# Sorting stage of a graph network kernel: one-hot compares in 16 bit, rows laid by value and then tile

## The reference

```python
edge_index = jnp.stack([src, dst])
x = x + _L0_gnn_ref(_layernorm(x, axis=-1), edge_index, ...)
...
x = x + _L1_gnn_ref(_layernorm(x, axis=-1), edge_index, edge_attr_256, ...)   # sums by dst
...
x = x + _L2_gnn_ref(_layernorm(x, axis=-1), edge_attr_20, ..., edge_index)    # sums by src
...
x = x + _L3_gnn_ref(_layernorm(x, axis=-1), edge_index, ...)                  # softmax and sums by dst
```

## Time and profile before

| | us |
|---|---|
| timed runs | 4594.09, 4598.11, 4608.26 (median 4598.11) |
| span of the profiled execution, first to last instruction | 4590.3 |
| median above that span | 7.8 |
| sorting stage, from the start to the next stage's first loads | 0 to 487.7 |
| first stretch, counting list 0 | 20.8 to 101 |
| second stretch, ranking list 0 and counting list 1 | 113 to 318 |
| third stretch, ranking list 1 | 322 to 460 |
| POOL's scatters in this stage | 118.9 to 483.0 |

### The profile page before, as it was taken

One profiled execution on the slowest core, in us unless ns is written; L12 is line 12 of the kernel. 1 busy time (PEld: TensorE's weight loads), 2 busy tenths in 40 slices (PEclk: granted clock), 3 DMA queues, 4 the chain that ended last, 5 costly groups with the idle time before them and its releaser, 6 DMA issues. The chain is left out here.

```text
span 4590.3 us, 75478 instructions
## 1 busy us (share of the span) xinstructions
PE 3650.0 (80%) x20805; PEld 2939.0 (64%) x20890; DVE 2883.1 (63%) x6152; ACT 1718.4 (37%) x3863; POOL 2500.7 (54%) x2542
## 2 busy tenths in 40 slices
PE   5779369879999999834299999479999678887288
PEld 4666257667788888633288888367777566666165
DVE  8887359348889899652288888433333445554753
ACT  2667332302333333212167767243333223333132
POOL 5887547667777777366377777200000277775300
PEclk9655579889999999857599999779999878888589
DMA  9456426349999999644378888310000167776400
GB/s 197 142 184 208 124 86 202 120 155 310 328 331 337 335 337 336 196 117 143 116 216 247 249 239 238 115 65 1 0 0 0 51 177 210 211 211 193 115 15 28
DMA packets 661729, 790.38 MB, mean 172 GB/s; under 512 B 151811, under 2 KB 584051, under 8 KB 657812
## 3 DMA queue, kind: packets, MB, share of 16 engines
q1 hardware_dynamic: 369553, 300.43, 22.4%
q0 software_dynamic: 117920, 308.04, 22.2%
q10 hardware_dynamic: 174083, 179.76, 12.9%
HBM read 516.89 MB, written 275.42 MB: 173 GB/s over the span
## 5 line engine op out<-in xcount | busy, mean ns | idle before, releaser
L1593 POOL DMA_INDIRECT by_dst<-dst_row,place x416 | 462.4, 1112 | 167.5 <-issue 113.5
L2776 POOL DMA_INDIRECT fl_far<-x_table,fl_index x416 | 448.7, 1079 | 150.4 <-issue 126.5
L2187 POOL DMA_INDIRECT a_far<-kv_table,a_index x416 | 428.1, 1029 | 156.3 <-issue 119.4
L2508 POOL DMA_INDIRECT a_far<-src_table,a_index x416 | 415.9, 1000 | 132.0 <-issue 121.0
L2813 PE MATMUL ps<-fl_w,fl_hid 128*128 128x256 f32 x1664 | 399.5, 383 | 17.7 <-ACT ps L2885 16.8
L3609 POOL DMA_INDIRECT starts<-p_out,p_at x25 | 24.6, 984 | 705.3 <-DMA starts<-p_zero 697.4
L2221 PE MATMUL ps<-a_w,a_edge_t 128*128 128x256 f32 x1664 | 396.2, 381 | 0.0
L2813 PEld LDWEIGHTS ps<-fl_w,fl_hid 128*128 128x128 f32 x1664 | 310.3, 191 | 61.3 <-issue 21.3
L2221 PEld LDWEIGHTS ps<-a_w,a_edge_t 128*128 128x128 f32 x1664 | 302.0, 191 | 32.9
L1220 ACT ACTIVATE f_hid<-ps,f_bn 128x320 f32<-128x320 f32 x320 | 197.6, 618 | 327.4 <-PE ps L1174 327.4
L1261 DVE SCALAR_TENSOR_TENSOR x_sb<-ps,f_cw,x_sb 128x256 f32 x200 | 96.8, 484 | 343.4 <-PE ps L1185 343.4
(11 more groups left out here) (581 smaller groups left out, 9330.7 us busy)
## 6 DMA issues: line engine op xcount, KB each, us to landing
partial<-a_out ACTq DMA_DIRECT2D x208, 546.0 KB
a_edge<-by_dst SPq DMA_DIRECT2D x104, 516.0 KB
partial_f<-fl_out ACTq DMA_DIRECT2D x26, 2056.0 KB
dst_row<-in_edge_attr SPq DMA_DIRECT2D x52, 1024.0 KB
xn_sb<-q_table SPq DMA_DIRECT2D x416, 128.0 KB
fl_keys<-key_rows SPq DMA_DIRECT2D x26, 1024.0 KB, 5.2
a_keys<-local_rows SPq DMA_DIRECT2D x104, 128.0 KB
m_far<-kv_table SPq DMA_DIRECT2D x15, 640.0 KB, 7.2
```

Of the source, the lines that this page charges most:

```text
L1593: self.nc.gpsimd.indirect_dma_start(out=self.table, out_offset=bass.IndirectOffsetOnAxis(ap=self.place[:, n:n + 1], axis=0), in_=self.row[ ...
L2187: gathered[b % 4].count(nc.gpsimd.indirect_dma_start(out=far[:, b, u, :], out_offset=None, in_=kv_table, in_offset=bass.IndirectOffsetOnAx ...
L2508: gathered[b].count(nc.gpsimd.indirect_dma_start(out=far[:, b, u, :], out_offset=None, in_=src_table, in_offset=bass.IndirectOffsetOnAxis( ...
L2776: gathered[q * 4 + t // 4].count(nc.gpsimd.indirect_dma_start(out=far[:, q, t, :], out_offset=None, in_=table, in_offset=bass.IndirectOffs ...
```

## The change

`split` becomes bf16 (its values, up to 127, are exact there). Two new tiles hold the numbers to compare with, written once: `every_lo` (each of 128 values eight times) and `every_hi` (each of 25 values eight times), both bf16. `lo_hot`, `hi_hot` and `hit` turn from tile, value to value, tile. In the three compares the key operand was one number repeated along a row (step 0) and the other fp32; now the key operand is eight neighbouring bf16 numbers, repeated from the outside, and all operands are bf16. The readers follow: a weight tile `lo_hot[:, h % 2, :, m]` and a moving tile `hi_hot[:, h % 2, :, m]` are now read with eight elements (16 bytes) from one to the next, and `take` reads `hit` so too. No instruction changes its place; two casts are added at the start of DVE's work.

```diff
@@ -1698,10 +1698,11 @@
     with Stage(core, "place") as st:
         nc, ps = core.nc, core.ps
         raw = ends[:].rearrange("p s n -> p (s n)").bitcast(I32).rearrange("p (s n) -> p s n", s=2)
-        split = st.sb("split", [P, 2, 2, ETILES])
-        lo_hot = st.sb("lo_hot", [P, 2, 8, P], BF16)
-        hi_hot = st.sb("hi_hot", [P, 2, 8, W], BF16)
-        hit = st.sb("hit", [P, 2, 8, W], BF16)
+        split = st.sb("split", [P, 2, 2, ETILES], BF16)
+        every_lo, every_hi = st.sb("every_lo", [P, P, 8], BF16), st.sb("every_hi", [P, W, 8], BF16)
+        lo_hot = st.sb("lo_hot", [P, 2, P, 8], BF16)
+        hi_hot = st.sb("hi_hot", [P, 2, W, 8], BF16)
+        hit = st.sb("hit", [P, 2, W, 8], BF16)
         bits = st.sb("bits", [P, 4, 32, UNITS, 4], BF16)
         bits_t = st.sb("bits_t", [P, 2, CHUNKS, 512], BF16)
         ident = st.sb("ident", [P, P], BF16)
@@ -1788,8 +1789,8 @@
                     pe.wait_ge(lo_made, h + 1)
                     pe.wait_ge(hi_made, h + 1)
                     for m in range(8):
-                        last = nc.tensor.matmul(ps[:, HIST[h % 2], m * W:HB].rearrange("p (n a) -> p n a", a=W), lo_hot[:, h % 2, m, :],
-                                                hi_hot[:, h % 2, m, :].unsqueeze(1).broadcast_to([P, 8 - m, W]),
+                        last = nc.tensor.matmul(ps[:, HIST[h % 2], m * W:HB].rearrange("p (n a) -> p n a", a=W), lo_hot[:, h % 2, :, m],
+                                                hi_hot[:, h % 2, :, m].unsqueeze(1).broadcast_to([P, 8 - m, W]),
                                                 start=(m == 0), stop=(m == 7), skip_group_check=True)
                     last.then_inc(counted, 1)
 
@@ -1915,6 +1916,8 @@
                 ch.add(nc.vector.tensor_scalar(cut[:, 1], raw[:], 7, None, ALU.logical_shift_right))
                 ch.settle()
                 ch.link(nc.vector.tensor_copy(split[:], cut))
+                ch.add(nc.vector.tensor_copy(every_lo[:], core.c("iota").unsqueeze(2).broadcast_to([P, P, 8])))
+                ch.add(nc.vector.tensor_copy(every_hi[:], core.c("iota25").unsqueeze(2).broadcast_to([P, W, 8])))
                 ch.add(nc.vector.tensor_copy(ident[:], core.c("ident")))
                 for u in range(4):
                     ch.add(nc.vector.tensor_scalar(lo_bits[:, u], core.c("lo_bits"), core.c("strip")[:, u:u + 1], None, ALU.mult))
@@ -1948,10 +1951,10 @@
                         make_bits(s * 2 + g // (2 * UNITS))
                     if h >= 2:
                         dve.wait_ge(counted, h - 1)
-                    nc.vector.tensor_tensor(lo_hot[:, h % 2], core.c("iota").unsqueeze(1).broadcast_to([P, 8, P]),
-                                            split[:, 0, s, g * 8:g * 8 + 8].unsqueeze(2).broadcast_to([P, 8, P]), ALU.is_equal).then_inc(lo_made, 1)
-                    nc.vector.tensor_tensor(hi_hot[:, h % 2], core.c("iota25").unsqueeze(1).broadcast_to([P, 8, W]),
-                                            split[:, 1, s, g * 8:g * 8 + 8].unsqueeze(2).broadcast_to([P, 8, W]), ALU.is_equal).then_inc(hi_made, 1)
+                    nc.vector.tensor_tensor(lo_hot[:, h % 2], every_lo[:], split[:, 0, s, g * 8:g * 8 + 8].unsqueeze(1).broadcast_to([P, P, 8]),
+                                            ALU.is_equal).then_inc(lo_made, 1)
+                    nc.vector.tensor_tensor(hi_hot[:, h % 2], every_hi[:], split[:, 1, s, g * 8:g * 8 + 8].unsqueeze(1).broadcast_to([P, W, 8]),
+                                            ALU.is_equal).then_inc(hi_made, 1)
 
                 def find_begins(s):
                     dve.wait_ge(kept, (s + 1) * G)
@@ -1984,7 +1987,7 @@
                     dve.wait_ge(looked, h + 1)
                     dve.wait_ge(ranked, h + 1)
                     ch.settle()
-                    ch.link(nc.vector.tensor_tensor(picked, ps[:, SEL[h % 2], 0:HB].rearrange("p (t a) -> p t a", a=W), hit[:, h % 2], ALU.mult))
+                    ch.link(nc.vector.tensor_tensor(picked, ps[:, SEL[h % 2], 0:HB].rearrange("p (t a) -> p t a", a=W), hit[:, h % 2].rearrange("p a t -> p t a"), ALU.mult))
                     ch.link(nc.vector.tensor_reduce(before, picked, AX, ALU.add))
                     ch.link(nc.vector.tensor_tensor(place[:, s, g * 8:g * 8 + 8], ps[:, SEL[h % 2], RANK], before, ALU.add))
                     dve.sem_inc(taken, 1)
@@ -2003,8 +2006,7 @@
                             take(s, g - 1)
                         if g < G:
                             h = s * G + g
-                            ch.add(nc.vector.tensor_tensor(hit[:, h % 2], core.c("iota25").unsqueeze(1).broadcast_to([P, 8, W]),
-                                                           split[:, 1, s, g * 8:g * 8 + 8].unsqueeze(2).broadcast_to([P, 8, W]), ALU.is_equal))
+                            ch.add(nc.vector.tensor_tensor(hit[:, h % 2], every_hi[:], split[:, 1, s, g * 8:g * 8 + 8].unsqueeze(1).broadcast_to([P, W, 8]), ALU.is_equal))
                     if s == 0:
                         nc.vector.memset(core.x[:, TILES - 1, :], 0.0).then_inc(padded, 1)
 
```

## The result

The changed kernel takes 4633.11 us (median of six runs, 4617.77 to 4638.12) against 4607.09 for the kernel before, timed beside it: ratio 1.0056, 95% interval 1.0041 to 1.0071. It is slower by some 26 us, where 50 us less were forecast. The profiled spans say the same: 4615.3 (the changed kernel's run of 4617.77) against 4590.3.

The account below looks back on a forecast made before the run. GpSimd's scatters, by late start and slow first half, were taken to bound the sorting stage; its end moves from 484.6 to about 433, held by GpSimd and the PE chain, counted as 50 us off 4598.1: 4548, own range 4533 to 4565.

Parts of the forecast that it names:

- the counting matmuls: PE's L1791, eight per group: 0.76 us now, forecast unchanged with 16 bytes between streamed elements; bounds 0 to perhaps factor 2.
- The weight row: PE transposes loading key bits at a 104-byte step, 0.11 us apart; taken as evidence that the streamed step costs 0.
- R1: Slower rival: moving tile's 16-byte step costs PE two array steps per column, counting 1.51 for 0.76 us; 4621 us; chance 0.17.
- A: Sorting stretch 20 to 101 us, counting the first list; forecast 1.05 us per group for 1.41, ending 18 us earlier.
- B: Sorting stretch 113 to 318 us, ranking list one beside counting list two; forecast 12 us gained, ending 30 us earlier.
- C: Sorting stretch 322 to 460 us, ranking list two; forecast as it is, VectorE having a quarter of its time free.
- The compares: VectorE's three one-hot compares at two elements per step: L1951 1.22 to 0.69 us, each of the two short ones to 0.26.
- GpSimd's start: First row scatter in the sorting stage: forecast at 105.5, 13.4 us earlier, held by the dst_row load instead of VectorE.
- GpSimd's pace in B: Time per item of eight scatters while one-hot rows are made: forecast 11.2 us, range 10.6 to 12.4, against 13.7.
- R4: PE's clock rises through fewer gaps, VectorE bounds A and B: 4552 us, inside the forecast's range; chance 0.55 together with forecast.
- R3: Rival: compares no faster, casts and strided take add 1.4 and up to 8 us: 4595 to 4612 us; chance 0.08.
- the scatter model: Scatters at 1.29 us against a compare closing 1.1 us in every 3.57 give 14.28 us per item, claimed to match the trace.

Follow-up runs that it names:

- e1: Changed kernel with the moving tile hi_hot back by tile then value (2-byte step), lo_hot and hit left spread: 4553.33 us, 0.9909 of the kernel before.
- e5: Changed kernel with hi_hot in fours of tiles, 8 bytes between streamed elements: 4542.75 us, 0.9899 of the kernel before.
- e8: Changed kernel with both hi_hot buffers between each other, 32 bytes between streamed elements: 4618.22 us in one run, 1.0067 of the kernel before.
- e6: e1 with every eighth group's hi_hot (13 groups) at 16-byte step in its own tile: 4549.97 us in one run, 0.9918 of the kernel before.
- e4: Changed kernel with hi_hot in pairs of tiles, 4 bytes between streamed elements: 4552.72 us, 0.9911 of the kernel before.
- e7: Changed kernel with only lo_hot in the new order, hi_hot and hit as in the kernel before: 4549.21 us, 0.9914 of the kernel before.
- e2: Changed kernel with the weight tile lo_hot back by tile then value, hi_hot still at 16 bytes: 4618.63 us, 1.0055 of the kernel before.

## Why the prediction was wrong, and where it was right

**The step that failed** is the price of the counting matmuls: "I take 0, nearest to the weight row of the same engine". The weight row said truly what weights cost at that level (e1: 0.98 against 0.96), and says nothing of the streamed operand. The upper bound, "on PE perhaps 2", was too low as well: 0.76 became 1.66, a factor of 2.2, beyond the 1.7 from which the prediction let the rival decide.

**R1 is what happened.** It gave A 16 us, B 32 us and a chain that ends at 507.5, for 4621, 23 us above the kernel before. Measured: the first scatter 23 us later, the chain 57 us later (23 in A, 34 in B, none in C), at 516.3, and 26 us above the kernel before, which itself took 9 us more here (4607.09) than in the runs from which the prediction began (4598.11). A costs 1.85 per group where R1 had 1.73, as the group's matmuls take 1.66 and not 1.51. The range was cut at 4613, inside R1; with R1 in full it would have ended at 4630, still short of the 4633 measured. The chance of 0.17 followed from the same fault: the one row of a long step read by a datapath, L1959 at 1.7, and PE at 9.33 of 10 us both spoke for R1, and against it stood only a row of another operand and the argument that PE streams at half its top rate.

**That argument would have held, but for the size.** A fixed time for each stretch does hide behind a slow clock, nearly so at 8 bytes in e5; at 16 bytes its 1.83 ns exceed even the lower level's 0.84. The Trainium skill ("Advanced Engine Details and Errata", section "SBUF Cachelines") says that accesses which each fall in another 16-byte line are penalized, and e8, e5 and e6 agree with it for the moving operand, where more than one element in a line lowers the price; the weights of e1 do not show it at the lower level (0.98 against 0.96) and little at the higher (0.68 to 0.74 against 0.61).

**What was right**, each with its number:
- The compares: 0.69 and 0.26 forecast, 0.691, 0.255 and 0.267 measured.
- take: 0.15 us more forecast, 0.14 measured. The two casts: 1.4 forecast, 1.05 measured (0.69 and 0.35).
- GpSimd's start, once PE doesn't hold it: 105.5 behind the load of dst_row forecast, 107.9, 108.8 and 108.0 in e1, e4 and e7, with 12.05 us of idle that the load ended in e1. In e5 (106.2) the places held it.
- GpSimd's pace in B: 11.2 per item forecast; 10.8 in the changed kernel, 11.7 in e1 (14 items from 107.9 to 271.5).
- The sum without the price on PE: the stage 50 us shorter forecast, 40 in e1 and 47 in e5 (487.7 against 441.0). Of e1's missing 10 us, 2.4 are the start, and some 7 the pace (14 items at half a microsecond).

R4 came true in part: in e1 PE reaches the higher level in A (granted clock 0.90 over 30 to 81), and two of its groups there follow each other in 1.9 us; the stage's end is GpSimd's all the same, as the prediction said. R4's reason, fewer gaps, is not shown: in the changed kernel PE is busy for 10.00 of 10 us and stays at the lower level. R3 did not come.

**Readings that were off and decided nothing.** The mean clock of 0.65 over B counts its start up to 133 us, where nothing is recorded, as 1.00. From 133 to 318 it is 0.61, so two tenths of B ran at the higher level and not three; that gives some 11.5 us where 12 were taken. The 14.28 us per item that the scatter model gives is not "what stands in the trace": that was 13.7. And the 7.8 us between span and median are no fixed distance, since they compare different executions: the changed kernel's run of 4617.77 has a span of 4615.3.

## What to carry to other kernels

A layout has a reader on each engine that touches it: before elements are moved apart for the one, price the step for the other, and take the streamed operand and the loaded weights as two different readers. Where the trace has no row of the very same reading, a row from next door is no reason to take zero; the bound at which the verdict turns (here 1.7) belongs beside it, and the engine that is nearly full says which way an unknown price will count. Here the cure is to spread only the tile that PE loads as weights, or to keep the streamed elements 4 or 8 bytes apart: e1, e4, e5 and e7 all beat the kernel before by about 1% and the changed one by about 1.5%.

## What the runs showed of the hardware

- A streamed bf16 element that begins a new 16-byte stretch costs PE 1.83 ns at either level of its clock (1.60 us over 875 columns; 1.82 and 1.83 us per counting row in e6); at 32 bytes the row takes 1.85 (e8), against 1.84 at 16.
- With two elements to a stretch the counting row takes 1.04 us at the higher level and 1.08 at the lower (e5): such a stream gains nothing from a faster clock.
- Weights loaded at a step of 16 bytes cost next to nothing at the lower level (0.98 us per counting row in e1 against 0.96 in the kernel before) and 0.07 to 0.13 us at the higher (0.68 to 0.74 against 0.61).
- In the changed kernel and in e2 and e8, where the strided stream fills PE, every row of L1804 in the stage takes 0.58 to 0.64 us, the duration that it has elsewhere at 0.50 (0.59) and not at 1.00 (0.38); in e1 and e5, with less work on PE, stretches at 1.00 appear. Why is not settled by these runs.
